# Row scatters over seven stage buffers of shorter rows, and expert numbers packed four to a word

## What is computed

```
x = x + L0_xattn(LN(x), k, bias, ctx, ctx)      # a causal convolution of products v*x2, over 8 heads
x = x + L0_ffn(LN(x))                           # dense layer and 16 low-rank experts, top 2
x = x + L1_xattn(LN(x), ctx)                    # attention of 16 heads, int8-like rounding of q and o
x = x + L1_ffn(LN(x))                           # 32 experts, top 4, and a shared expert:
    scores = sqrt(softplus(flat @ router_w.T)); idx = top_k(scores + expert_bias, 4)
    out += p[:, e] * (silu(clip(x @ wg[e].T)) * clip(x @ wu[e].T)) @ wd[e].T    for the 4 chosen e
```

## Time and profile before

| | us |
|---|---|
| median of 3 runs | 776.68 |
| lowest, highest | 773.65, 780.56 |
| the profiled execution | 783.03 |
| its span | 781.2 |
| PE busy, share of the span | 600.9, 77% |
| DVE, ACT, POOL busy | 511.7, 356.5, 376.5 |
| mean granted clock of TensorE | 0.893 of 2.4 GHz |

### The profile page before, as it was taken

How to read it: one execution, slowest core, us unless ns; L and a number is a source line. 1 busy time by engine, 2 the same in 40 slices (tenths; PEclk the granted TensorE clock), 3 DMA queues, 4 the chain that set the end, 5 groups by cost and what they waited for, 6 DMA issues and landing times.

```text
span 781.2 us, 14111 instructions
## 1 busy us (share of the span) xinstructions
PE 600.9 (77%) x4045; PEld 480.6 (62%) x4045; DVE 511.7 (65%) x1554; ACT 356.5 (46%) x1010; POOL 376.5 (48%) x526
## 2 busy tenths in 40 slices
PE   1579999999789888789986684681689898898930
PEld 1578777877567677678754452570567676676810
DVE  1647767778887667875668436671367684555787
ACT  1013556566746456635687454420234353443510
POOL 6687654654534778623372025332145453444550
PEclk9999999999989999889998675596799998989975
DMA  8999999999999433101343924952344343434669
GB/s 292 237 352 350 349 349 347 344 341 323 333 342 328 129 114 115 37 27 36 92 142 116 396 93 142 328 183 77 110 130 130 110 144 115 151 102 130 189 236 297
DMA packets 135674, 159.37 MB, mean 204 GB/s; under 512 B 15184, under 2 KB 124880, under 8 KB 135344
## 3 DMA queue, kind: packets, MB, share of 16 engines
q1 hardware_dynamic: 113312, 113.90, 47.7%
q10 hardware_dynamic: 14656, 23.20, 8.4%
q0 software_dynamic: 7632, 21.37, 7.5%
HBM read 54.73 MB, written 104.24 MB: 203 GB/s over the span
## 4 chain that ended last, share of the span: by engine, by line
PE 31%; SPq 29%; DMA 14%; issue 10%; DVE 8%; POOL 4%; ACT 3%; ACTq 0%; DVEq 0%; POOLq 0%
SPq L1347 26%; PE ps L605 8%; PE pS L577 5%; DMA stage<-xn_rows 3%; DMA expert_rows<-stage,ixl 3%; DMA expert_rows<-stage 3%; PE pc L556 2%; POOL y_rows L1320 2%; DMA stage<-in_pad 2%; DMA y_rows<-tk,work 2%; SPq L1330 2%; DVE xs L1040 2%; PE ps L522 2%; PE pS L536 2%; DMA work<-y_rows 1%
## 5 line engine op out<-in xcount | busy, mean ns | idle before, releaser
L1320 POOL DMA_INDIRECT y_rows<-tk,work x95 | 96.8, 1019 | 112.4 <-ACT tk L1228 95.0
L556 PE MATMUL pc<-arena,tk 128*128 128x128 f32 x768 | 104.3, 289 | 16.7 <-DVE arena L773 9.6
L556 PEld LDWEIGHTS pc<-arena,tk 128*128 128x128 f32 x768 | 97.6, 203 | 19.8 <-DVE arena L773 13.3
L605 PE MATMUL ps<-arena,work 128*128 x380 | 104.6, 400 | 0.2 <-ACT work L1223 0.2
L1296 POOL TENSOR_TENSOR arena<-arena 128x512 f32<-128x512 f32 x64 | 89.8, 1420 | 11.1 <-ACT arena L1101 11.0
L1310 POOL DMA_INDIRECT expert_rows<-stage,ixl x64 | 63.9, 998 | 59.0 <-DMA stage<-xn_rows 41.8
L577 PE MATMUL pS<-arena,tk 128*128 x190 | 64.9, 425 | 20.9 <-issue 18.5
L1166 ACT ACTIVATE work<-pS,work 128x128 f32<-128x128 f32 x256 | 72.8, 373 | 11.0 <-DVE work L791 10.5
L972 DVE TENSOR_SCALAR work<-ps 128x256 f32<-128x256 f32 x95 | 40.2, 423 | 54.3 <-PE ps L605 51.5
L605 PEld LDWEIGHTS ps<-arena,work 128*128 128x128 f32 x380 | 69.3, 203 | 6.7 <-issue 0.6
L1218 ACT ACTIVATE tk<-work 128x128 f32<-128x128 f32 x95 | 29.4, 310 | 84.0 <-DVE work L972 67.2
(11 more groups left out here) (273 smaller groups left out, 1411.0 us busy)
## 6 DMA issues: line engine op xcount, KB each, us to landing
expert_rows<-stage SPq DMA_DIRECT2D x32, 2176.0 KB, 20.7
work<-expert_rows SPq DMA_DIRECT2D x95, 130.0 KB
arena<-in_w ACTq DMA_DIRECT2D x8, 1536.0 KB, 13.3
stage<-xn_rows SPq DMA_DIRECT2D x64, 136.0 KB
xn_rows<-xnD ACTq DMA_DIRECT2D x16, 512.0 KB
work<-y_rows SPq DMA_DIRECT2D x16, 512.0 KB, 5.1
tk<-in_tk SPq DMA_DIRECT2D x1, 2048.0 KB, 9.4
out<-xs SPq DMA_DIRECT2D x16, 128.0 KB, 2.8
```

What stands on the lines that cost most here:

```text
L556: i = pe.matmul(pv, tk[:, h, 128 * d:128 * d + 128], kvv[:, ci, :, :].rearrange("p b (i h j) -> p (b i) h j", i=8, h=8)[:, :, hl, :], star ...
L605: i = pe.matmul(p[U * k:U * k + U, 0:256], xgT[n % 3][:, 128 * c + U * k:128 * c + U * k + U], arena[:, 256 * c:][:, bass.ds(e, 256)], sta ...
L1320: pool.indirect_dma_start(out=Yr, out_offset=bass.IndirectOffsetOnAxis(ap=xg[n % NX][:, 256:257].bitcast(U32), axis=0), in_=y[n % 4], in_o ...
```

## The change

Rows of `xn_rows` and `expert_rows` have 260 words instead of 272. There are seven stage buffers (`NS`) instead of four; to make room, `regs` and `pk4` move into a part of `tk` that is free by then. `d_list` and `d_y` become one set of semaphores, `d_sc`, and `d_w` and `d_xr` lose one each. The expert numbers are no longer written one to a word, times 768, but four to a word, five bits each: word i holds tiles i, i + 24, i + 48 and i + 72. PE loads the NW = 24 words once, by two loads of 12, after the shared expert and ahead of the loop, and takes a tile's number out by a shift and a mask. The multiplication by 768 moves into the address arithmetic. Most ticks of the five tables change.

```diff
-ROW = 272
+ROW = 260
+NS = 7
+NW = -(-NT // 4)
...
-        XR = [0] * 8 + [1] * 4 + [2] * 2
-        XV = [32] * 8 + [16] * 6
+        XR = [0] * 8 + [1] * 6
+        XV = [32] * 14
...
-        stage = sb("stage", [128, 4, ROW])
+        stage = sb("stage", [128, NS, ROW])
...
+        regs = tk[0:1, 5, 0:5 * NW].bitcast(I32)
+        pk4 = tk[:, 5, 192:256].rearrange("p (b k) -> p b k", k=KT)
...
-        d_st = [sem(f"d_st{i}") for i in range(4)]
-        d_list = [sem(f"d_list{i}") for i in range(4)]
-        d_w = [sem(f"d_w{i}") for i in range(2)]
+        d_st = [sem(f"d_st{i}") for i in range(NS)]
+        d_sc = [sem(f"d_sc{i}") for i in range(NS)]
+        SC = [-(-(KT * NB - i) // NS) for i in range(NS)]
+        d_w = sem("d_w")
...
-            "S": 971, "tab": 3371, "conv": 404, "oP": 1124}
+            "S": 979, "tab": 3348, "conv": 411, "oP": 1132}
...
-            "xc": 1117, "list": 1899}
+            "xc": 1114, "list": 1918}
...
-            breg = [[pe.alloc_register(f"base{i}_{j}") for j in range(WR)] for i in range(2)]
+            word = [pe.alloc_register(f"base{j}") for j in range(NW)]
             base = {}
             pe.wait_ge(s_regs, 2)
+            for i in range(0, NW, 12):
+                pe.load(word[i:i + 12], regs[0:1, 4 * NW + i:4 * NW + i + 12])
+            word = [pe.snap(r, min_val=0, max_val=NE ** 4 - 1) for r in word]
             pe.wait_ge(s_acc, NB)
             for t in range(NT + 6):
-                if Q * t % WR == 0 and t < NT:
-                    w = min(WR, Q * (NT - t))
-                    half = breg[Q * t // WR % 2]
-                    pe.load(half[:w], regs[0:1, Q * (NT + t):Q * (NT + t) + w])
-                    for j in range(w // Q):
-                        base[t + j] = [pe.snap(half[Q * j + k], min_val=0, max_val=768 * (NE - 1)) for k in range(Q)]
+                if t < NT:
+                    field = (word[t % NW] >> 5 * (t // NW)) & 31
+                    base[t] = [pe.snap(field * 768, min_val=0, max_val=768 * (NE - 1))]
...
                 for m in at(t, T_DVE["te"], 1, 2):
+                    p = place["regs", m]
                     dve.wait_ge(s_rwP, m + 1)
-                    dve.tensor_copy(regs[0:1, Q * NT * m:Q * NT * m + Q * NT].rearrange("o (t q) -> o q t", q=Q),
-                                    place["regs", m][0:1, 0:Q * NT].rearrange("o (q t) -> o q t", q=Q)).then_inc(s_regs, 1)
+                    if m == 0:
+                        dve.tensor_copy(regs[0:1, 0:4 * NW], p[0:1, 0:4 * NW]).then_inc(s_regs, 1)
+                    else:
+                        dve.tensor_copy(ecol[0:1, :], p[0:1, 0:4 * NW]).then_inc(*own.up())
+                        dve.wait_ge(*own.now())
+                        for k in range(2, -1, -1):
+                            o = regs[0:1, 4 * NW:5 * NW] if k == 0 else ecol[0:1, NW * k:NW * k + NW]
+                            i = dve.scalar_tensor_tensor(out=o, in0=ecol[0:1, NW * (k + 1):NW * (k + 2)], scalar=float(NE),
+                                                         in1=ecol[0:1, NW * k:NW * k + NW], op0=ALU.mult, op1=ALU.add)
...
-                        pool.wait_ge(d_st[j % 4], 16 * (j // 4 + 1))
+                        pool.wait_ge(d_st[j % NS], 16 * (j // NS + 1))
                         pool.indirect_dma_start(
                             out=Xs, out_offset=bass.IndirectOffsetOnAxis(ap=ixl[:, b, k:k + 1], axis=0),
-                            in_=stage[:, j % 4, :], in_offset=None).then_inc(d_list[j % 4], 16)
+                            in_=stage[:, j % NS, :], in_offset=None).then_inc(d_sc[j % NS], 16)
...
-                        if j >= 4:
-                            sp.wait_ge(d_list[j % 4], 16 * (j // 4))
-                        sp.dma_start(stage[:, j % 4, :], Xd[k, 128 * b:128 * b + 128, :]).then_inc(d_st[j % 4], 16)
+                        if j >= NS:
+                            sp.wait_ge(d_sc[j % NS], 16 * (j // NS))
+                        sp.dma_start(stage[:, j % NS, :], Xd[k, 128 * b:128 * b + 128, :]).then_inc(d_st[j % NS], 16)
```

More of the change, by code:

```diff
@@ L244, in build @@
             sem(n) for n in ("d_pk", "d_tk", "d_qp", "d_zero"))
-        d_st = [sem(f"d_st{i}") for i in range(4)]
-        d_list = [sem(f"d_list{i}") for i in range(4)]
-        d_w = [sem(f"d_w{i}") for i in range(2)]
+        d_st = [sem(f"d_st{i}") for i in range(NS)]
+        d_sc = [sem(f"d_sc{i}") for i in range(NS)]
+        SC = [-(-(KT * NB - i) // NS) for i in range(NS)]
+        d_w = sem("d_w")
         d_xn = [sem(f"d_xn{i}") for i in range(2)]
         d_g = [sem(f"d_g{i}") for i in range(4)]
-        d_y = [sem(f"d_y{i}") for i in range(4)]
         d_r = [sem(f"d_r{i}") for i in range(4)]
         s_tm, s_t5, s_thr, s_x5P, s_x5 = (sem(n) for n in ("s_tm", "s_t5", "s_thr", "s_x5P", "s_x5"))
-        d_xr = [sem(f"d_xr{i}") for i in range(3)]
+        d_xr = [sem(f"d_xr{i}") for i in range(2)]
         d_out = sem("d_out")
@@ L599, in tensor_program @@
                     if n == 0:
[L600 to L601 removed]
+                        pe.wait_ge(d_w, 16 * NE // 4)
                     pe.wait_ge(s_gT, n + 1)
@@ L952, in vector_program @@
                 for m in at(t, T_DVE["te"], 1, 2):
+                    p = place["regs", m]
                     dve.wait_ge(s_rwP, m + 1)
-                    dve.tensor_copy(regs[0:1, Q * NT * m:Q * NT * m + Q * NT].rearrange("o (t q) -> o q t", q=Q),
-                                    place["regs", m][0:1, 0:Q * NT].rearrange("o (q t) -> o q t", q=Q)).then_inc(s_regs, 1)
+                    if m == 0:
[7 more added lines that the diff above has]
+                                                         in1=ecol[0:1, NW * k:NW * k + NW], op0=ALU.mult, op1=ALU.add)
+                            if k:
+                                i.then_inc(*own.up())
+                                dve.wait_ge(*own.now())
+                            else:
+                                i.then_inc(s_regs, 1)
             key4 = key[:, :, 0:KT]
@@ L1225, in scalar_program @@
                     if n >= 4:
-                        act.wait_ge(d_y[n % 4], 16 * (n // 4))
+                        act.wait_ge(d_sc[n % 4], 16 * (SC[n % 4] + n // 4))
                     act.wait_ge(s_yp, n + 1)
@@ L1340, in sync_program @@
             sp.wait_ge(d_id, 16)
-            sp.dma_start(stage[:, :, :], a_pad).then_inc(d_id, 16)
+            sp.dma_start(stage[:, 0:4, :], a_pad).then_inc(d_id, 16)
             sp.wait_ge(d_id, 32)
             sp.dma_start(Xs[NE * NB * 128:(NE * NB + 4) * 128, :].rearrange("(c p) d -> p c d", p=128),
-                         stage[:, :, :]).then_inc(d_zero, 16)
+                         stage[:, 0:4, :]).then_inc(d_zero, 16)
             for t in range(TICKS):
@@ L1367, in sync_program @@
                 if n == 0:
-                    for i in range(4):
-                        sp.wait_ge(d_list[i], 16 * NB)
+                    for i in range(NS):
+                        sp.wait_ge(d_sc[i], 16 * SC[i])
                 if n >= 4:
@@ L1372, in sync_program @@
                 if n >= NX:
-                    sp.wait_ge(d_y[(n - NX) % 4], 16 * ((n - NX) // 4 + 1))
+                    sp.wait_ge(d_sc[(n - NX) % 4], 16 * (SC[(n - NX) % 4] + (n - NX) // 4 + 1))
                 for k in range(Q):
```

29 lines of the change are left out of this document (13 added, 16 removed), and 16 rows, old and new, of tables (T_ACT, T_DVE, T_PE).

## The result

The changed kernel took 746.36 us (median of 4 runs, 743.92 to 748.61) beside 776.30 for the kernel before (4 runs). The ratio is 0.961, 95% interval [0.955, 0.967]: 30 us faster. The forecast was 730 us with a range of 716 to 747. The direction and the range hold; 16 us of the forecast gain did not come. In a later set of runs two executions of the kernel before took 1184 and 1453 us; they are left out of its median there.

What follows compares the result with a forecast made beforehand. PE bounds most of the kernel, apart from scatter latency before the loop and register-load pauses in it. 28.0 + 16.2 + 2.2 = 46.4 us off 783.03 gives 736.6; less 6.3 for a slow profiled execution, 730 us, range 716 to 747.

Steps and rivals of the forecast that it cites:

- The register loads: Tile loop: five pauses at PE's loads of 16 registers, and the half clock behind them, go; 28.0 us gained.
- the unpacking: Tile loop: 166 register operations that take out expert numbers, hidden behind queued products; taken as zero.
- The loop's start: Between shared expert and first transposes: scatters end earlier, PE's register load comes last; 16.2 us gained.
- from 530.0 us that ends at 536.9: Ahead of the loop: PE's 24 words take 6.45 us plus three unpackings, ending where 553.10 stood.
- The shorter rows: SP's fills of expert_rows: 4.4% smaller, so they end earlier and PE waits less; 2.2 us gained.
- If time follows bytes: Assumption for SP's 32 fills: 4.4% fewer bytes make them end 9.4 us earlier.
- Fills take as long as before: Sign at SP's fills that the forecast would be wrong: no shorter than 6.66 us each.
- The moved ticks: Start ticks, with a few neighbours changing places: taken as zero, with 9 us on both sides.
- Exposed arithmetic: Rival, tile loop: PE's added sequencer steps are not hidden and take back 25.7 us; 756 us, chance 0.06.
- a DMA-bound tail: Rival, last scatters: DMA engines busy with weights, loop starts some 10 us later; 740 us, chance 0.08.
- a supply that can't keep 1.67 us a tile: Rival, tile loop: SP's gathers fall behind without pauses and half the gain goes; 744 us, chance 0.09.
- The rival of slower rows: Rival, SP's fills and scatters: rows straddling 64-byte boundaries write slower; 796 us, slower than before, chance 0.04.

Runs made afterwards that it cites:

- the words alone: Kernel before with only the packed expert numbers, loaded once ahead of the loop; 272-word rows, four buffers and old ticks kept: 751.92 us, ratio 0.968.
- the set where no result of PE came late: Changed kernel run again without further change, beside the kernel before on another chip: 733.32 us, ratio 0.946.
- the third set: Later runs on a chip of their own, with the changed kernel repeated unaltered (748.05 us, ratio 0.961) beside variants of it and the kernel before.

## Why the prediction was right, and where it was wrong

**The register loads: 28.0 us forecast, 27.1 in the loop, 23 in the run of the words alone.** The mechanism holds, with the half clock behind each pause, and the unpacking cost nothing, as taken. The size is that of one slow execution: the profiled loop of before took 190.3 us, but 186.8 and 186.2 with short rows or new ticks and the same six loads. The forecast took 6.3 us off its sum for that execution, so the total holds better than the term. What the forecast did not see is that 0.27 us a register is not the price of a register load: it is the price of one that starts at 380 + 64 i bytes. The hint stood in the trace: SP's loads of 16 from the start of the same buffer took 1.0 to 1.5 us. I never put the two side by side.

**The loop's start: 16.2 us forecast, 9.3 measured.** The step "from 530.0 us that ends at 536.9" failed twice, in opposite directions. The two loads were priced at 6.45 us and took 1.9. And the 530.0 was copied from the profile of before, as if the shared expert would stay where it was; it ended at 541.6. The forecast named the register load as what comes last, in truth it is the shared expert, which had been hidden for 22 us and had no slack left once the scatters were early. In the set where no result of PE came late the loop starts at 531.09, earlier than forecast, and the kernel takes 733 us. That the 730 comes near it is partly luck: the loads were priced 4.5 us too high, and the rows had the wrong sign. That 746 lies inside the range that reaches to 747 is luck too: the range was widened for rivals that do not show.

**The shorter rows: 2.2 us forecast, 8 to 9 us lost by themselves.** "If time follows bytes" was wrong: 32 fills take 205.7 us instead of 205.8. "Fills take as long as before" was among the forecast's own signs of being wrong, and it came. The doubt that the prediction worked out as an estimate from the Trainium skill's "DMA: Bandwidth & Descriptors" (How a descriptor splits into AXI transactions), that a short row at any multiple of 16 bytes costs about as much as a longer one at multiples of 64, agrees with that equality, though the page's rule is for reads and these are writes. The loss itself was not in the sum at all: 8192 tails of 16 bytes, which make the fills and the first scatter 5 us late; the rest of the 8 to 9 us is not accounted for. I worked out what `ROW` does to the fills and left out the other DMA whose size hangs on it. With the new ticks POOL waits less at the first scatter, 2.45 us where it waited 8.98.

**The moved ticks: 0 with 9 us on both sides.** Zero with the kernel before, 7 us with the other changes in, as far as two overlapping intervals tell. Parts of a change that share a critical path don't add; the forecast priced each against the old path.

**The rivals.** Exposed arithmetic, a DMA-bound tail and a supply that can't keep 1.67 us a tile: none shows, though 746 is nearer to the 740 and 744 us of the last two than to 730. The loop is 162 to 164 us in every variant with words, and scatters go 1.27 us apart when a buffer is ready. The rival of slower rows had the right sign, but its place, fills above 8.1 us, was wrong.

## What to carry to other kernels

When a wait goes, look at everything that stood behind it unseen, and take its end from what it depends on, not from where the old trace has it; then ask how much it varies, since a hidden engine's hiccups come to light with it. When a size changes, list every transfer whose shape hangs on it, the small ones at the start too. And when one kind of instruction has two prices in one trace, find out why before building on either.

## What the runs showed of the hardware

A load of PE's registers costs 0.07 to 0.11 us a register, mostly 0.08, where it starts at a multiple of 16 bytes in its buffer (8, 12 and 16 registers: 0.60, 0.86 to 1.04, 1.15 to 1.60 us; the second load of 12 starts at byte 432), and 0.26 to 0.27 us a register from 380 + 48 i or 380 + 64 i bytes (12 and 16: 3.14 and 4.30 us, medians). Whether 16 bytes or 8 is the bound was not tried. The Trainium skill's "Runtime: NRT & Kernel Launch" (Instruction fetch mechanics) gives about 200 ns a register for loads; these runs have both a dearer and a much cheaper one, and the measurement decides.

8192 pieces of 16 bytes, at multiples of 16, written from memory to memory took 17.5 to 18.4 us in seven profiles, 8192 of 64 bytes at multiples of 64 took 13.5 to 13.8 in seven. Rows of 1040 bytes at multiples of 16 filled memory in the same time as rows of 1088 at multiples of 64, 6.64 and 6.66 us for 2048 of them.

In the first measurement and in the third set results of PE came up to 4.7 us late between 515 and 533 us, with no DMA and no wait in the records to explain it, and at a granted clock of 1.00 from 518 to 524 us; in the profiles of the other two sets they did not.
